# A decoder layer on one core: one shared order of work replaced by an order for each engine, DRAM round trips around the solve by DVE transposes, and resident expert weights by streamed ones

## The reference, cut to what matters

```
# 1: delta-rule attention, 16 heads of 16, per batch
q, k, v = x@Wq, x@Wk, silu(x@Wv);  q, k normalised per head;  beta = sigmoid(x@Wb)
for t in 256 tokens: S += k_t (beta_t (v_t - S^T k_t))^T;  o_t = S^T q_t
x = layernorm(x + (rms-normalised o * weight) @ Wo)
# 2: state-space block on ctx, gated by x, 256 channels, 16 states
u = silu(conv4(ctx @ in_proj));  dt, B, C = projections of u;  delta = softplus(dt)
for n in 16 states: h_n[t] = exp(delta_t A_n) h_n[t-1] + delta_t u_t B_n[t];  y += h_n C_n
x = layernorm(x + (y + D u) * silu(x))
# 3: experts: 2 shared, 16 routed (top 4 by sigmoid score), hidden size 176
x = layernorm(2 x + sum over experts e of g_e (relu(x @ w1_e + b1_e) @ w2_e + b2_e))
```

## Time and profile before

| | us |
|---|---|
| runs: median (lowest to highest of 3) | 664.37 (662.49 to 664.68) |
| profiled execution | 661.15 |
| its span, first to last instruction | 659.4 |
| PE busy | 453.7 (69%) |
| DVE busy | 371.7 (56%) |
| ACT busy | 235.4 (36%) |
| POOL busy | 188.2 (29%) |
| mean granted clock of PE | 0.794 of full |

### The profile page before, as it was taken

How to read it: one execution, slowest core, us unless ns; L and a number is a source line. 1 busy time by engine, 2 the same in 40 slices (tenths; PEclk the granted TensorE clock), 3 DMA queues, 4 the chain that set the end, 5 groups by cost and what they waited for, 6 DMA issues and landing times.

```text
span 659.4 us, 18772 instructions
## 1 busy us (share of the span) xinstructions
PE 453.7 (69%) x8414; PEld 316.8 (48%) x8414; DVE 371.7 (56%) x576; ACT 235.4 (36%) x425; POOL 188.2 (29%) x100
## 2 busy tenths in 40 slices
PE   5555338845856785883775453454798899999994
PEld 2323214512433452441563352443577777778883
DVE  2553677789837597788825552211465565353334
ACT  3445534422512655631445321124244322122220
POOL 2000023522621453551000000008444563333441
PEclk9676767975978798885877655655798999899998
DMA  8001010101000000101000015302300000000000
GB/s 261 2 1 30 5 31 21 21 1 33 2 4 3 3 0 3 31 8 33 3 3 3 19 20 168 105 3 84 119 1 1 0 1 1 1 32 1 1 1 32
DMA packets 27963, 18.07 MB, mean 27 GB/s; under 512 B 19873, under 2 KB 25835, under 8 KB 27627
## 3 DMA queue, kind: packets, MB, share of 16 engines
q1 hardware_dynamic: 27723, 16.84, 8.7%
q0 software_dynamic: 160, 0.04, 0.1%
HBM read 13.66 MB, written 3.21 MB: 26 GB/s over the span
## 4 chain that ended last, share of the span: by engine, by line
PE 36%; DVE 34%; ACT 12%; issue 10%; POOL 3%; DMA 2%; SPq 1%; DVEq 1%; POOLq 0%; ACTq 0%
PE bank L634 8%; DVE arena_h L1281 7%; PE bank L624 5%; DVE tmp_o L1326 5%; PE bank L838 3%; DVE arena_h L1290 3%; DVE tt_s L1327 3%; PE bank L833 2%; PE bank L813 2%; PE bank L834 2%; PE bank L814 2%; PE bank L815 2%; POOL hg_lo L561 2%; PE bank L658 2%; DVE hg_hi L1488 2%
## 5 line engine op out<-in xcount | busy, mean ns | idle before, releaser
L540 POOL TENSOR_TENSOR arena_s<-du,bsb 128x1024 f32<-128x1024 f32 x32 | 87.3, 2730 | 216.9 <-ACT bsb L960 186.1
L561 POOL TENSOR_TENSOR hg_lo<-vkp,hg_hi 128x512 fp32r<-128x512 f32 x50 | 69.0, 1380 | 92.1 <-DVE hg_hi L1488 92.1
L1281 DVE TENSOR_TENSOR_SCAN arena_h<-arena_s 128x1024 f32<-128x1024 f32 x32 | 80.6, 2517 | 9.1 <-POOL arena_s L540 6.6
L624 PE MATMUL bank<-arena_h,const 128*128 128x512 f32 x128 | 79.0, 750 | 2.9 <-DVEq L1292 2.9
L1484 DVE TENSOR_TENSOR vkp<-vkp,bank 128x512 f32<-128x512 f32 x50 | 34.4, 687 | 73.4 <-ACT vkp L1121 72.7
L1121 ACT ACTIVATE vkp<-bank,b 128x512 f32<-128x512 f32 x50 | 34.3, 686 | 110.2 <-PE bank L815 109.9
L634 PE MATMUL bank<-vkp,tiles 32*32 32x32 f32 (+1 forms) x3072 | 37.5, 200 | 28.6 <-issue 15.5
L547 POOL TENSOR_TENSOR w_lo<-w,w_hi 128x3200 fp32r<-128x3200 f32 x2 | 13.8, 6938 | 139.1 <-ACT w_hi L1059 139.1
L634 PEld LDWEIGHTS bank<-vkp,tiles 32*32 32x32 f32 x3072 | 34.3, 119 | 36.4 <-issue 21.6
L834 PE MATMUL bank<-w_lo,hg_hi 128*128 128x256 f32 x200 | 51.1, 287 | 0.0
L969 ACT ACTIVATE arena_s<-delta,negA 128x510 f32<-128x510 f32 x64 | 42.3, 711 | 16.9 <-DVEq L1282 16.9
(11 more groups left out here) (195 smaller groups left out, 843.9 us busy)
## 6 DMA issues: line engine op xcount, KB each, us to landing
w<-in_w SPq DMA_DIRECT2D x1, 3200.0 KB, 12.2
w<-in_w SPq DMA_DIRECT2D x3, 512.0 KB, 7.9
xT<-in_x_t SPq DMA_DIRECT2D x1, 1024.0 KB, 7.3
xres<-in_x_tok SPq DMA_DIRECT2D x1, 1024.0 KB, 8.9
scr_a<-at_g SPq DMA_DIRECT2D x4, 256.0 KB, 2.0
at_g<-scr_a SPq DMA_DIRECT2D x32, 32.0 KB, 2.0
scr_t<-tt_s SPq DMA_DIRECT2D x4, 256.0 KB, 2.0
at_g<-scr_t SPq DMA_DIRECT2D x32, 32.0 KB, 2.0
```

The source lines that it names most:

```text
L540: pool.tensor_tensor(dBu[:, i % 2, :].rearrange("p (e t) -> p e t", e=2), du[:, :, GT_ * th:GT_ * th + GT_], bsb[:, i % 2, :].unsqueeze(1) ...
L561: pool.tensor_tensor(hg_lo[i % 2][:, :], hrel[:, i % 2, :], hg_hi[i % 2][:, :], ALU.subtract).then_inc(s_hglo, 1)
L624: mm = pe.matmul(o[:, :], ident, hC[i % 2][:, GT_ * et:GT_ * et + GT_], start=(n == 0), stop=(n == DS - 1))
L1281: link(dve.tensor_tensor_scan(hst, dA[:, i % 2, :], dBu[:, i % 2, :], 0.0, ALU.mult, ALU.add))
```

## The change

Five things are changed; nothing else of the arithmetic is.

1. `order()` and `bank_turns()` give way to `Plan`: operations with an engine, a duration, what they come after and which PSUM banks they take and free. `play` lets all engines run by these durations, always takes the operation that can start first, and among equals the one with the longest way to the end. Each engine gets its own list. Batches 0 and 1 start together; batch b + 2 starts when batch b's normalised output is there.
2. `move_a` and `move_t` are gone; DVE turns the blocks itself into a buffer `a_own` and back.
3. Expert weights are brought in as 13 groups of two tiles from the start, split into `w_hl` (both parts), and stored to `scr_w` in DRAM. The experts read them through a ring of 8 tiles of 512 KB; each tile is fetched twice, once per half. A fetch waits until its ring place was used; the first eight wait until attention is over.
4. Scan buffers keep their memory through the experts, so scans may go on beside them. The ring, `x_hl` and `sel` lie on attention's buffers. The comparison buffers of the gates are now attention's `qke` for both halves, so routing of either half waits for the end of attention (`chain_end`).
5. Experts' output banks come from the play as all others; the second half's middle is placed by it too.

The diff, cut:

```diff
+RING = 8
+class Plan:
...
+    def play(self, fixed, begin):
...
+        for k in reversed(list(self.ops)):
+            us, lag = self.ops[k][:2]
+            way[k] = us + lag + max([way[n] for n in users[k]], default=0.0)
...
+        while open_:
+            ways = {k: choice(k) for k in open_}
+            k = min(open_, key=lambda k: (ways[k][0], -way[k]))
+            at, banks = ways[k]
...
+            self.order[k[0]].append(k[1:])
+            engine[k[0]] = at + us
...
+def attention(op, b, on, wo):
+    k = op("pe", "k", b, 2.2, on, takes=[("k", b)])
...
+    s = op("dve", "solve0", b, 5.6, [d])
+    s = op("dve", "solve1", b, 4.1, [s])
+    s = op("dve", "solve2", b, 7.4, [s, moved])
+    tile_t = op("act", "tile_t", b, 1.4, [s])
...
+    for h in range(2):
+        p = op("pe", f"UW{h}", b, 1.8, [p, a, vt], takes=[(f"UW{h}", b)])
...
+    for c in range(1, NREC + 1):
+        p = op("pe", f"S{c}", b, .45, [s, d])
+        s = op("act", f"S{c}", b, .25, [p], frees=[("H", b)] * (c == NREC))
...
+def work():
...
+    for g in range(NGRP):
+        before = [staged[g - 2][1]] if g >= 2 else []
+        r = op("sp", "wraw", g, .5, [before[0]] if before else [], lag=6.0)
+        h = op("act", "whi", g, 1.1, [r] + ([staged[g - 2][2]] if g >= 2 else []))
+        lo = op("pool", "wlo", g, 2.4, [h])
+        staged.append((h, lo, op("sp", "wst", g, .5, [lo], lag=6.0)))
...
+        dbu[i] = op("pool", "dbu", i, 2.75, [copy[i], dve_, scan.get(i - 2)])
+        scan[i] = op("dve", "scan", i, 2.5, [decay, dbu[i], add.get(i - 1)])
...
+    chain_end = [on[2], on[3]]
...
+        split = op("dve", "split", th, 1.3, [a])
+        p = op("pe", "gates0", th, 1.5, [a3, *chain_end, mid_done.get(th - 1)], takes=[("score", th)])
...
+            loads[i] = op("sp", "wload", i, .5, [*chain_end, outs.get(i - RING), *[s[2] for s in staged]], lag=4.0)
+            hid[i] = op("pe", "hid", i, 1.65, [loads[i], split, mid_done[th], sel, hid.get(i - 1)], takes=[("h", i), ("G", i)])
...
-                if name == "move_a":
-                    sp.wait_ge(s_at[x], 4 * (n + 1))
-                    sp.dma_start(scr_a[b], at_g[x][:, :]).then_inc(s_adram[x], 16)
...
+            def fetch_raw(g):
+                if g >= 2:
+                    sp.wait_ge(s_wlo, g - 1)
+                n = group(g)
+                sp.dma_start(w_raw[g % 2][:, 0:n.stop - n.start, :], w12_d[n].rearrange("f p n -> p f n")).then_inc(s_raw[g % 2], 16)
+            def keep(g):
+                sp.wait_ge(s_wlo, g + 1)
...
+            def fetch(i):
...
+                    sp.wait_ge(s_hguse, i - RING + 1)
+                sp.dma_start(w_ring[:, i % RING, :, :].bitcast(F32), scr_w[i % FT]).then_inc(s_wld[i % RING], 16)
...
+            def split_lo(g):
...
+                pool.tensor_tensor(w_hl[g % 2][:, 0:n, 1, :], w_raw[g % 2][:, 0:n, :], w_hl[g % 2][:, 0:n, 0, :],
+                                   ALU.subtract).then_inc(s_wlo, 1)
...
+            def split_hi(g):
...
+                act.wait_ge(s_raw[g % 2], 16 * (g // 2 + 1))
+                if g >= 2:
+                    act.wait_ge(s_kept[g % 2], 16 * (g // 2))
+                act.activation(w_hl[g % 2][:, 0:n, 0, :], w_raw[g % 2][:, 0:n, :], ACT.Copy).then_inc(s_whi, 1)
...
-                        dve.wait_ge(s_ain[x], 128 * (n + 1))
+                        dve.wait_ge(s_at[x], 4 * (n + 1))
+                        link(dve.transpose(a_own[x][:, :].rearrange("p (s g t) -> p t g s", s=C, g=CLO),
+                                           at_g[x][:, :].rearrange("p (h c t) -> p t h c", h=2, c=NC)))
...
-                        dve.nop().then_inc(s_tt[x], 1)
+                        dve.transpose(at_g[x][:, :].rearrange("p (h c t) -> p t h c", h=2, c=NC),
+                                      tt_s[x][:, :].rearrange("p (j g t) -> p t g j", j=C, g=CLO)).then_inc(s_turned[x], 1)
```

More of the change, by code:

```diff
@@ L73 @@
 GATE_PARTS = 8
[L75 to L106, removed]
@@ L512, in _ @@
[L512 to L521 removed]
+                sp.wait_ge(s_beta[x], n + 1)
@@ new lines, in output_bias @@
+            def output_bias(th):
+                for tt in range(4):
+                    mm = pe.matmul(out_bank(th, tt), gT[th][0:NX, P * tt:P * tt + P], b2[:, :], start=False, stop=True,
+                                   skip_group_check=True)
+                    if tt % 2:
+                        filled(("out", th, tt // 2), mm)
+            for name, which in order["pe"]:
+                if name == "xe":
+                    conv_input(which)
+                elif name == "dt_rows":
+                    dt_rows()
+                elif name == "dt":
+                    dt_all(which)
+                elif name == "B":
+                    broadcast_b(which)
+                elif name == "C":
+                    broadcast_c(which)
+                elif name == "sum":
+                    sum_states(which)
+                elif name == "yT":
+                    y_rows(which)
+                elif name == "x3T":
+                    x3_columns(which)
+                elif name[:5] == "gates":
+                    gates(which, int(name[5:]))
+                elif name == "hid":
+                    hidden(which)
+                elif name == "out":
+                    outputs(which)
+                elif name == "b2":
+                    output_bias(which)
+                else:
@@ L891, in _ @@
                     step(name, which)
-            for th in range(NG):
-                experts(th)
         @block.scalar
@@ new lines, in hidden_relu @@
+            def hidden_relu(i):
+                k = ("h", i)
+                o = take(k)
+                if i >= 2:
+                    act.wait_ge(s_hglo, i - 1)
+                signal(act.activation(hrel[:, i % 2, :], o[:, :], ACT.Relu, bias=b1[:, i % FT:i % FT + 1]),
+                       s_rel, i + 1, k)
+            for name, which in order["act"]:
+                if name == "xe":
+                    conv_rows(which)
+                elif name == "silu":
+                    silu(which)
+                elif name == "dtlo":
+                    dt_rows()
+                elif name == "dt":
+                    softplus(which)
+                elif name == "copy":
+                    copy_b(which)
+                elif name == "decay":
+                    decays(which)
+                elif name == "gate":
+                    gate(which)
+                elif name in ("yT", "nst"):
+                    rstd(MID)
+                elif name == "x3T":
+                    x3_columns(which)
+                elif name == "split":
+                    split_x3(which)
+                elif name[:5] == "gates":
+                    gates(which, int(name[5:]))
+                elif name == "whi":
+                    split_hi(which)
+                elif name == "relu":
+                    hidden_relu(which)
+                else:
```

884 lines of the change are left out of this document (435 added, 449 removed), and 4 rows, old and new, of the table ATTENTION.

## The result

The changed kernel takes 653.5 us (median of 4 runs, 652.6 to 654.8) against 663.5 us (4 runs, 662.5 to 664.7) for the kernel before beside it: a ratio of 0.985, interval 0.982 to 0.988. The forecast was 545. So 10 us came of the 119 expected. The profiled run has a span of 653.0.

What follows compares the result with a forecast made beforehand. No engine was full: attention's tail was waiting, scans shared a DVE-POOL lock, PE paced the experts. First expert tile 350 + experts 181 + tail 9.4 = 540.4, + 1.75 = 542, median 3.2 higher: 545 us; range 510 to 600.

Steps and rivals of the forecast that it cites:

- 304 + 18 + 8 = 330: End of attention: 304 us DVE and lock bound, 18 for weight splits, 8 for misfits, giving 330 us.
- 8 us misfit: Attention: 8 us added for in-order queue waits, orders not fitting true durations, and small-matmul blocks slower than planned.
- The path of one batch: Attention bound: 130 us a batch beside scans, two batches in a row from 14 us on, 274 us.
- DVE's ledger with the lock: Attention bound: work passing DVE and the lock shared with POOL, 292 us from 12 us on, 304 us.
- Transposes: Solve's DRAM round trips become DVE transposes of 0.71 us each, saving about 14 us on the last batch's path.
- Splits: Early expert-weight splits on POOL before attention's end: 31 us of work, 15 to 20 us of cost taken.
- Gates gap: Between attention's end and the first expert tile: serial routing, 20 us with little PE work, first tile at 350 us.
- the cost of a tile: Experts: PE takes 3.24 us a tile, 50 tiles 162 us; 181 us with additions.
- E: Order buys nothing; only round trips (14 us) and late splits (about 10) go: 640 us; chance 0.05.
- B: Attention: splits hold DVE up for all 31 us, 25 us more queue misfit, end at 368: 583 us; chance 0.22.
- C: Experts: weight tiles stream at the slower row, 4.45 us each, 51 us more: 596 us; chance 0.08.
- D: Experts: weight loads land one at a time, 7.9 us a tile, 196 us more: 741 us; chance 0.05.

Runs made afterwards that it cites:

- grouped kernels: Changed kernel with each small matmul of six attention stages run over the columns of four or of two chunks: 557.1 and 586.3 us.
- e5_group4: Changed kernel with each small matmul in P, UW, H, GQ, base and O run over four chunks' columns, a quarter of the matmuls: 557.1 us, ratio 0.839.
- e12_group4_stagger: Changed kernel with the edits of e5_group4 and e1_stagger together: 555.7 us, ratio 0.837.
- e1_stagger: Changed kernel with one plan edge added: attention of batch 1 waits until ScalarE has copied state 7 of batch 0; 622.4 us, ratio 0.939.
- e7_no_split: Changed kernel without GpSimd's 13 splits of expert weights; ScalarE writes the high half twice instead: 648.2 us, ratio 0.977.
- e4_quarter: Changed kernel with four 32x32-tile matmuls per chunk replaced by one over all 128 rows with identity weights: 800.2 us, ratio 1.209.

## Why the prediction was wrong

- **The step that failed** is the end of attention, "304 + 18 + 8 = 330". The row of it was read, 768 small matmuls in 24 us with up to 2.8 us of issue waits, and it went into the sum as part of an 8 us misfit. What the runs showed in its place: PE is handed 32 pairs a microsecond, and by the grouped kernels the number of its small matmuls costs the new order 96 us. Of the 108 us between 545 and 653.5 that leaves 12: e5_group4 takes 557.1 us. There attention ends at 342, with 330 forecast, and the first expert tile starts at 373, with 350 forecast.
- **Two bounds, and the third left out.** The path of one batch (274) and DVE's ledger with the lock (304) were both worked out; PE had no ledger, and the prediction noted that no engine was full. (The path holds some of the shortage, as its last 59 us were measured with the waits in them; but it wasn't the bound that was taken.) At 32 pairs a microsecond the 6,080 pairs (UW, GQ and base 3,072, P and O 1,984, H 1,024) alone take 190 us of the queue, by an estimate from that pace. They have the 360 us of scans and solves (80.9 to 441) to hide in, but only if they are spread.
- **What "batches 0 and 1 start together" does.** The prediction named this edge and gave it no price. It is harmless when instructions are plentiful (e12_group4_stagger: 1.4 us) and costs 31 us when they are not (e1_stagger).
- **Transposes:** 14 us on the path was right, 13.5 measured, each 1.07 us and not 0.71. In the old order 7 to 9 us of it reach the end; the solve came later, and ACT's queue held the turned matrix back.
- **Splits:** 18 us forecast, about 5 measured. In e7_no_split the first scan starts at 77.52 and takes 2.28 us, against 80.92 and 4.24: so they delay it by 3.4 us and lengthen it by 1.96. The other 7.5 us by which it misses 70 aren't theirs: du, which the forecast had at the old kernel's place or earlier (73.78), is done at 78.25, and without splits at 74.85.
- **Gates gap:** 20 forecast, 31 measured (441.0 to 472.1). The three scans at 442.39, 447.06 and 462.77 and the three C multiplications beside them take 12.1 us of it. The prediction had put the late scans into the experts. These are 11 us shorter than forecast, and up to 50 x (3.24 - 3.05) = 9.5 us of that is the cost of a tile, which was read too high. What answers to the earlier trace rows (timeline, DVE):

```profile
447.06 3.10 DVE L1350 TENSOR_TENSOR_SCAN arena_h<-arena_s 128x1024 f32<-128x1024 f32 x1 [0.21 <-DVE arena_h L1359]
...
450.57 1.22 DVE L1515 TENSOR_TENSOR qke<-sc 128x1024 f32<-128x1024 f32 x1
...
462.77 2.29 DVE L1350 TENSOR_TENSOR_SCAN arena_h<-arena_s 128x1024 f32<-128x1024 f32 x1 [0.22 <-DVE arena_h L1359]
465.28 0.69 DVE L1543 CAST stk<-bank 96x512 bf16<-96x512 f32 x1 [0.22 <-DVE arena_h L1350]
```

  The scores' routing stands behind one scan, its copies behind another.

- **The rivals.** E, "the order buys nothing", gave 640 and is the nearest in time, with 0.05. Its reason, that a batch's path stays as long and the same holes stay open, comes near, but the holes are new ones. B asked for 25 us of queue misfit and had the kind right and the size wrong by four. C and D fell: PE waited for no load.

What stays open: how much of the 96 us is waiting and how much the lower clock that comes with it. Why half and quarter of the pairs give an even price and no threshold was not tested further, nor what sets the pace of 32 a microsecond. Of the 23 us between 350 and 373 in e5_group4, 12 are there at the end of attention, where the first scan is 10 late (79.82), and 11 are the gates gap. Larger tiles (64 rows, half the instructions for the same result) were not tried.

## What to carry to other kernels

Make a ledger of instructions beside the ledger of busy time. Small matmuls in long rows can be bound by how fast they are handed over (here 32 pairs a microsecond), and this profile shows it as "issue" in waits of equal length between runs of equal count. A planner that let two like batches start together set their like stages side by side; one edge that keeps the second back until state 7 of the first gave three times what the whole change had given.

## What the runs showed of the hardware

- PE was handed 254 pairs in 8.03 us, in runs of 127 to 128 of 1.9 us with 1.5 to 2.2 us between, whatever the columns (16 or 32). The instruction queue moved 11 packets of 16 KB in that stage, for 3,104 instructions.
- Within a run the pairs go by at 1.93 / 127 = 15 ns each. The shortage halves the pace.
- In the stretches with these waits the granted clock is 0.50 to 0.56; with a quarter of the pairs, in the same window (126.8 to 171), 0.89.
- f32 matmuls over 128 rows and columns of weights, with 32 columns of data, follow each other at 0.217 us with their weight loads (e4_quarter); 32x32 tiles go by at 31 ns with the shortage in.
- A DVE transpose of 128x512 f32 takes 0.71 us in one layout and 1.06 to 1.11 us in the two used here.
- A DVE product of two SBUF operands and a POOL operation held each other up: 2.03 us beside splits against 0.32 without them.
